# Direction attention: the second scores' banks handed over in pairs of heads, odd jobs between the pairs

## The chip, the cores and the metric

The program runs on one core of one Trainium2 chip, and the metric is the device time of one execution in microseconds. The core has a matrix engine (TensorE, PE in the profile), whose weight loads are a row of their own (PEld), a vector engine (VectorE, DVE), an activation engine (ScalarE, ACT), GpSimd (POOL), and a queue for transfers (SyncE, SP). TensorE writes to PSUM only, here eight banks of 512 fp32 columns on 128 partitions.

## The reference, cut to what matters

The model is four layers, each an attention block and a feed-forward block, each with a residual and a layer norm behind it. Only the attention of layer 1 is touched ("direction attention", `_L1_attn_ref`): 4 batches of 512 tokens, 8 heads, a causal softmax.

```
q3 = (x @ Wq.T).reshape(Bb, Tt, H, 3).transpose(0, 2, 1, 3)
k3 = (x @ Wk.T).reshape(Bb, Tt, H, 3).transpose(0, 2, 1, 3)
v = (x @ Wv.T).reshape(Bb, Tt, H, HD).transpose(0, 2, 1, 3)
scores = einsum('bhtd,bhsd->bhts', q3, k3) * scale + q_on_dir[..., :, None] * k_on_dir[..., None, :]
attn = softmax(where(causal, scores, -inf), axis=-1)
out = einsum('bhts,bhsd->bhtd', attn, v) ... @ Wo.T
```

The head's width for scores is 3, with a fourth product along a fixed direction; for values it is 16.

## The kernel before, in words

Each block is written with one instruction stream per engine, in an order written out by hand; engines wait for each other on semaphores, and each engine runs its stream strictly in the order of the text. Nothing is scheduled by a planner.

The stage is `direction_attention` (line 1749). Its inputs are `q_parts` and `k_parts`: bf16 parts of queries and keys, 32 rows per head, so that four heads fill 128 partitions. The work goes by 8 **units** U (4 batches by 2 groups of 4 heads), each of 4 **steps** k, one for each block of 128 keys; in all 32 steps s. There are two passes over the scores:

- **The first pass** finds the row maxima. It goes head by head (32 heads f, one per step, 7 heads ahead: in step s it is head s + 7). `first_mask` (line 1809) writes the causal mask into bank 0, 512 columns; `first_products` (line 1818) adds four diagonal products, then two long products into bank 1, then two "edge" products into bank 7. VectorE reduces the three in turn (`maxima`, lines 1962, 1964, 1966: "diagonal", "long", "edge"). After every fourth head it splits the maxima into bf16 parts (lines 1970 to 1974).
- **The second pass** makes the probabilities. `second(s)` writes the transposed scores less the maxima of four heads into banks 2 to 5: four products of 32 rows and (4 - k) x 128 columns (line 1851), one per head, then four products of 128 rows and 128 columns that add the mask (line 1854). ScalarE takes them in two exponentials of two banks each (`probabilities(s, 0)` and `(s, 1)`, line 1922), then `values(s)` (line 1865) multiplies by the values, four fp32 products into bank 6.

Three **odd jobs** share bank 7 with the edge products, so each waits until VectorE has reduced the edge of the head before: `spread_sums` (line 1872) in step k = 1, `max_rows` (line 1837) in step k = 2, `out` (line 1878) in step k = 0 of units 3, 5 and 7. `m_read` holds what bank 7 waits for. At the end of a unit ScalarE copies bank 6 out (`copy_y`, line 1928), and the next unit's first values wait for that copy. `less_maxima` (line 1979) makes the next unit's query operand from what `max_rows` wrote.

In step s TensorE runs: `second(s+1)`, `first_mask`, an odd job if there is one, `values(s)`, `first_products`. In the last 7 steps there is no first pass left.

The functions that the change touches, with the line numbers of the profile:

Of the kernel before, what the change touches and what calls it, by code (L numbers as in the profile page):

```python
# [1748 lines left out]
def direction_attention(core, q_parts, k_parts, v_aug, w_out, sum_spread, out_loaded):  # L1749
# [3 lines left out]
    H = 4  # L1753
    n_units = 2 * B
    n_steps = n_units * QT
    n_heads = n_units * H
    LEAD = 7
    with Stage(core, "a1") as st:
# [20 lines left out]
        def diagonal_done(f):  # L1779
            return 3 * f + 1  # L1780

        def long_done(f):
            return 3 * f + 2

        def edge_done(f):
            return 3 * f + 3

        def out_of(s):

            U, k = s // QT, s % QT  # L1790
            return (U - 3) // 2 if k == 0 and U >= 3 and U % 2 == 1 else None

        with nc.Block() as block:
            @block.gpsimd
            def _(pool):
                nc.gpsimd.memset(nparts[:], 0.0).then_inc(zeroed, 1)
                for U in range(n_units):
                    b, g = U // 2, U % 2
                    pool.wait_ge(inv_ready, U + 1)
                    if b > 0:  # L1800
                        pool.wait_ge(out_done, b)
                    nc.gpsimd.tensor_tensor(yn[:, g, :], y[:, g, :], inv_sum[:], ALU.mult).then_inc(yn_ready, 1)

            @block.tensor
            def _(pe):
                def first_mask(f):
                    if f >= 1:
                        pe.wait_ge(top_ready, diagonal_done(f - 1))
                    nc.tensor.matmul(ps_d, core.identb[:], mask_wide[:].rearrange("p q n -> p (q n)"), start=True, stop=False, skip_group_check=True)

                def first_products(f, m_read):

                    U, h = f // H, f % H
                    col, g = (U // 2) * T, U % 2
                    rows = slice(32 * h, 32 * h + 32)

                    def product(to, q, k, n):
                        return nc.tensor.matmul(to, q_parts[rows, g, col + q * P:col + (q + 1) * P], k_parts[rows, g, col + k * P:col + (k + n) * P],
                                                start=k != q, stop=True, skip_group_check=True)

                    for q in range(QT):
                        last = product(ps_d[:, q * P:(q + 1) * P], q, q, 1)
                    last.then_inc(first_ready, 1)
                    if f >= 1:
                        pe.wait_ge(top_ready, long_done(f - 1))
                    product(ps_f[:, 0:2 * P], 2, 0, 2)
                    product(ps_f[:, 2 * P:4 * P], 3, 1, 2).then_inc(first_ready, 1)
                    if m_read is not None:
                        pe.wait_ge(*m_read)
                    product(ps_m[:, 0:P], 1, 0, 1)  # L1830
                    product(ps_m[:, P:2 * P], 3, 0, 1).then_inc(first_ready, 1)

                def max_rows(U, m_read):
                    pe.wait_ge(nparts_ready, U + 1)
                    pe.wait_ge(*m_read)
                    for t in range(QT):
                        last = nc.tensor.matmul(ps_m[:, t * P:(t + 1) * P], nparts[:, t, :, :].rearrange("p h r -> p (h r)"), core.identb[:],
                                                start=True, stop=True)
                    last.then_inc(rows_ready, 1)

                def second(s):
                    U, k = s // QT, s % QT
                    col, g = (U // 2) * T, U % 2
                    size = (QT - k) * P
                    if k == 0:
                        pe.wait_ge(q_ready, U + 1)
                    if s > 0:
                        pe.wait_ge(probs_ready, 2 * (s - 1) + 2)
                    for h in range(H):
                        rows = slice(32 * h, 32 * h + 32)  # L1850
                        nc.tensor.matmul(ps_s[:, h, 0:size], k_parts[rows, g, col + k * P:col + (k + 1) * P], q_less[rows, g, k * P:T],
                                         start=True, stop=False, skip_group_check=True)
                    for h in range(H):
                        last = nc.tensor.matmul(ps_s[:, h, 0:P], core.maskb[:], core.identb[:], start=False, stop=True, skip_group_check=True)
                        if h % 2 == 1:
                            last.then_inc(s_ready, 1)

                def values(s):
                    U, k = s // QT, s % QT
                    b, g = U // 2, U % 2  # L1860
                    pe.wait_ge(probs_ready, 2 * s + 2)
                    if k == 0 and U > 0:
                        pe.wait_ge(y_ready, U)
                    for h in range(H):
                        last = nc.tensor.matmul(ps_y[32 * h:32 * h + 32, k * P:T], v_aug[:, b * QT + k, H * g + h, :], probs_t[:, s % 2, h, 0:(QT - k) * P],
                                                start=k == 0, stop=k == QT - 1, skip_group_check=True)
                    last.then_inc(values_done, 1)

                def spread_sums(U, m_read):
                    pe.wait_ge(y_ready, U + 1)  # L1870
                    pe.wait_ge(*m_read)
                    nc.tensor.matmul(ps_m, sum_spread[:], y[:, U % 2, :], start=True, stop=True).then_inc(sums_ready, 1)

                def out(b, m_read):
                    pe.wait_ge(yn_ready, 2 * b + 2)
                    pe.wait_ge(*m_read)
                    for g in range(2):
                        last = nc.tensor.matmul(ps_m, w_out[:, g, :], yn[:, g, :], start=g == 0, stop=g == 1)
                    last.then_inc(out_done, 1)

                pe.wait_ge(mask_ready, 1)
                pe.wait_ge(out_loaded, 2 * 16)
                m_read = None
                for f in range(LEAD):
                    first_mask(f)
                    first_products(f, m_read)
                    m_read = top_ready, edge_done(f)
                max_rows(0, m_read)
                m_read = q_ready, 1
                second(0)  # L1890
                for s in range(n_steps):
                    U, k, f = s // QT, s % QT, s + LEAD
                    if s + 1 < n_steps:
                        second(s + 1)
                    if f < n_heads:
                        first_mask(f)
                    if out_of(s) is not None:
                        out(out_of(s), m_read)
                        m_read = sum_done, out_of(s) + 1
                    if k == 1 and U >= 1:  # L1900
                        spread_sums(U - 1, m_read)
                        m_read = ln_ready, U
                    if k == 2 and U + 1 < n_units:
                        max_rows(U + 1, m_read)
                        m_read = q_ready, U + 2
                    values(s)
                    if f < n_heads:
                        first_products(f, m_read)
                        m_read = top_ready, edge_done(f)
                spread_sums(n_units - 1, m_read)  # L1910
                out(B - 1, (ln_ready, n_units))
# [642 lines left out]
```

## Time and profile before

| | us |
|---|---|
| median of 3 runs | 1914.7 |
| lowest and highest of them | 1914.29 and 1924.76 |
| the profiled execution, its own time | 1913.05 |
| its span, first to last instruction | 1910.9 |
| mean granted TensorE clock over the span | 0.931 |
| PE busy, share of the span | 87% |
| ACT, DVE, POOL busy | 59%, 58%, 38% |

The span runs from the first to the last instruction of the profiled execution, 2.15 us less than its own time. The shares of busy time are averages over all blocks of the model. The steps of the stage that is changed, from the first to the last of its matmuls in line 1851 and what follows them, lie between 286.6 and about 391 us of the span. A matmul of fp32 operands shows as two records.

### The profile page before, as it was taken

The page shows a single profiled execution, that of the slowest core. Times are in us where ns is not written, and L with a number is a line of the kernel's source. Part 1 is how long each engine was busy: PE and PEld are TensorE (multiplying, and loading weights), DVE is VectorE, ACT ScalarE, POOL GpSimd, SP SyncE. Part 2 cuts the span into 40 slices and gives each one's busy share as a digit, 9 for nine tenths or more (in the row PEclk, how much of TensorE's full clock was granted, in tenths as well). Part 3 has the DMA queues.
Part 4 walks back from the last instruction along what each step waited for, and adds up shares of the span by engine and source line. Part 5 has one row for each costly group of instructions (what it writes and reads, how often), then busy time and mean ns, then how long its engine had stood idle before and what let it go on. Part 6 is the DMA issues. An engine that isn't in the chain of part 4 may idle for free. (4 is left out here: it accounts for less than half of the span.)

```text
span 1910.9 us, 27976 instructions
## 1 busy us (share of the span) xinstructions
PE 1657.7 (87%) x8908; PEld 1061.3 (56%) x8908; DVE 1107.7 (58%) x2224; ACT 1125.7 (59%) x2356; POOL 735.3 (38%) x665
## 2 busy tenths in 40 slices
PE   5558978859999699999869999999989998858898
PEld 3337733328886466666435555555547886323685
DVE  5955675545655455555345555555548886652475
ACT  4324555537777355555456566556538887753687
POOL 1224420122332466666245545555424442001463
PEclk8868979969999899999979999999989999878899
DMA  1007200002121222222211111111117652000321
GB/s 40 1 14 171 65 1 1 1 27 92 73 82 60 54 59 61 56 60 62 67 41 38 45 44 37 43 45 40 29 35 279 221 213 81 1 0 20 111 105 45
DMA packets 54507, 120.43 MB, mean 63 GB/s; under 512 B 12788, under 2 KB 23900, under 8 KB 47196
## 3 DMA queue, kind: packets, MB, share of 16 engines
q1 hardware_dynamic: 54364, 118.68, 20.9%
q8 instruction: 70, 1.15, 0.2%
q14 instruction: 73, 0.60, 0.1%
HBM read 82.99 MB, written 2.10 MB: 45 GB/s over the span
## 5 line engine op out<-in xcount | busy, mean ns | idle before, releaser
L847 DVE TENSOR_TENSOR e_lo<-psum,e_hi 128x512 fp32r<-128x512 f32 x296 | 203.0, 686 | 90.8 <-ACT psum L812 90.7
L1459 ACT ACTIVATE h_probs<-psum,h_nmax 128x512 f32<-128x512 f32 (+3 forms) x256 | 132.6, 523 | 132.7 <-DVE h_nmax L1537 78.1
L1537 DVE TENSOR_REDUCE h_nmax<-psum 128x1 f32<-128x512 f32 (+3 forms) x256 | 113.9, 486 | 118.7 <-PE psum L1348 118.4
L770 PE MATMUL psum<-f_x_hi,f_w_hi 128*128 128x512 f32 x400 | 160.3, 401 | 6.8 <-DVE e_gated L861 4.0
L772 PE MATMUL psum<-f_x_lo,f_w_hi 128*128 128x512 f32 x400 | 158.9, 397 | 0.0
L771 PE MATMUL psum<-f_x_hi,f_w_lo 128*128 128x512 f32 x400 | 158.5, 396 | 0.0
L1274 POOL TENSOR_TENSOR h_swapped<-h_swapped,rope_tables 128x512 f32<-128x512 f32 x64 | 81.7, 1276 | 185.2 <-DMA h_swapped<-h_raw 185.2
L812 ACT ACTIVATE psum<-psum,f_b 128x512 f32<-128x512 f32 x200 | 132.4, 662 | 25.5 <-PE psum L772 25.5
L789 PE MATMUL psum<-e_lo,f_w_hi 128*128 128x512 f32 x364 | 143.8, 395 | 2.2 <-DVE e_lo L847 1.2
L786 PE MATMUL psum<-e_hi,f_w_hi 128*128 128x512 f32 x364 | 143.4, 394 | 0.0
L787 PE MATMUL psum<-e_hi,f_w_lo 128*128 128x512 f32 x364 | 143.1, 393 | 0.0
L1459 ACT ACTIVATE a_probs<-psum,a_nmax 128x512 f32<-128x512 f32 (+3 forms) x128 | 67.4, 527 | 118.1 <-DVE a_nmax L1537 69.5
L738 POOL TENSOR_TENSOR e_lo<-e_gated,e_hi 128x512 fp32r<-128x512 f32 x59 | 76.1, 1289 | 140.0 <-ACT e_hi L824 140.0
L732 POOL TENSOR_TENSOR sum_fm<-e_part,sum_fm 128x512 f32<-128x512 f32 x60 | 77.3, 1288 | 132.2 <-DVE e_part L873 97.3
L1274 POOL TENSOR_TENSOR a_swapped<-a_swapped,a2f_a_tables 128x512 f32<-128x512 f32 x64 | 83.0, 1296 | 109.4 <-DMA a_swapped<-a_raw 109.3
L1345 PE MATMUL psum<-h_k,h_q 64*128 64x384 f32 (+3 forms) x512 | 104.9, 485 | 22.0 <-DVE h_p_t L1546 16.8
L1355 PE MATMUL psum<-ident,h_probs 128*128 128x128 f32 x640 | 109.2, 279 | 0.4 <-ACT h_probs L1459 0.4
L1537 DVE TENSOR_REDUCE a_nmax<-psum 128x1 f32<-128x512 f32 (+3 forms) x128 | 62.6, 489 | 67.6 <-PE psum L1348 66.4
L818 ACT ACTIVATE e_hi<-psum 128x512 fp32r<-128x512 f32 x128 | 76.7, 599 | 39.1 <-PE psum L772 39.1
L1345 PE MATMUL psum<-a_k,a_q 128*128 128x512 f32 (+3 forms) x256 | 91.2, 438 | 6.6 <-DVE a_wvo L1529 6.6
L770 PEld LDWEIGHTS psum<-f_x_hi,f_w_hi 128*128 128x128 f32 x400 | 76.5, 191 | 25.8 <-issue 4.7
L1373 PE MATMUL psum<-h_p_t,h_v 128*64 128x256 f32 (+3 forms) x512 | 89.9, 451 | 0.0
(426 smaller groups left out, 4050.6 us busy)
## 6 DMA issues: line engine op xcount, KB each, us to landing
e_gate<-gates SPq DMA_DIRECT2D x46, 1024.0 KB, 4.7
a_swapped<-a_raw SPq DMA_DIRECT2D x128, 128.0 KB, 2.3
h_swapped<-h_raw SPq DMA_DIRECT2D x256, 64.0 KB, 2.0
e_gate<-gates SPq DMA_DIRECT2D x16, 512.0 KB, 6.7
f_w<-in_l_experts SPq DMA_DIRECT2D x8, 512.0 KB, 5.4
f_w<-in_l_experts SPq DMA_DIRECT2D x32, 128.0 KB, 4.6
e_gate<-gates SPq DMA_DIRECT2D x12, 256.0 KB, 4.2
f_w<-in_l_experts SPq DMA_DIRECT2D x9, 256.0 KB, 4.8
```

What stands on the lines that cost most here:

```text
L770: nc.tensor.matmul(to, w_h, ex.x_hi[:, cols(b)], start=True, stop=False, skip_group_check=True)
L771: nc.tensor.matmul(to, w_l, ex.x_hi[:, cols(b)], start=False, stop=False, skip_group_check=True)
L772: nc.tensor.matmul(to, w_h, ex.x_lo[:, cols(b)], start=False, stop=True, skip_group_check=True).then_inc(hid_ready, 1)
L786: nc.tensor.matmul(to, w_h, hi[:, n % PLACES, :], start=start, stop=False, skip_group_check=True)
L787: nc.tensor.matmul(to, w_l, hi[:, n % PLACES, :], start=False, stop=False, skip_group_check=True)
L789: nc.tensor.matmul(to, w_h, lo[:, n % PLACES, :], start=False, stop=True, skip_group_check=True).then_inc(out_done, 1)
L812: nc.scalar.activation(to, hidden_bank(n), ex.act_func, **bias(n)).then_inc(act_ready, 1)
L847: nc.vector.tensor_tensor(lo[:, n % PLACES, :], whole, hi[:, n % PLACES, :].bitcast(F32), ALU.subtract).then_inc(lo_dve, 1)
L1274: nc.gpsimd.tensor_tensor(swapped[:, j, :], swapped[:, j, :], tables[:, 2 * j + 1, :], ALU.mult).then_inc(sin_ready, 1)
L1345: nc.tensor.matmul(ring[j % RING][:, 0:(q + 1) * P], qs[rows, U % 3, q * P:(q + 1) * P], ks[rows, U % 3, 0:(q + 1) * P], start=True, stop= ...
L1459: nc.scalar.activation(probs[:, j % 4, 0:(q + 1) * P], ring[j % RING][:, 0:(q + 1) * P], ACT.Exp, bias=nmax[:, j % 8:j % 8 + 1], accum_out ...
L1537: nc.vector.tensor_reduce(nmax[:, j % 8:j % 8 + 1], ring[j % RING][:, 0:(q + 1) * P], AX.X, ALU.max, negate=True).then_inc(max_ready, 1)
```

## The change

`second` now takes a pair number p as well: it makes the products and masks of heads 2p and 2p + 1 only, and waits only for the one exponential that read these two banks in the step before. The main loop issues pair 0 at the start of the step, then the odd job, then pair 1, then the values; `first_mask` moves from ahead of the odd job to behind the values, straight ahead of `first_products`. ScalarE's, VectorE's and GpSimd's instructions and waits are unchanged.

```diff
-                def second(s):
+                def second(s, p):
...
-                    if k == 0:
+                    if k == 0 and p == 0:
                         pe.wait_ge(q_ready, U + 1)
                     if s > 0:
-                        pe.wait_ge(probs_ready, 2 * (s - 1) + 2)
-                    for h in range(H):
+                        pe.wait_ge(probs_ready, 2 * (s - 1) + p + 1)
+                    for h in range(2 * p, 2 * p + 2):
                         rows = slice(32 * h, 32 * h + 32)
...
-                    for h in range(H):
+                    for h in range(2 * p, 2 * p + 2):
                         last = nc.tensor.matmul(ps_s[:, h, 0:P], core.maskb[:], core.identb[:], start=False, stop=True, skip_group_check=True)
-                        if h % 2 == 1:
-                            last.then_inc(s_ready, 1)
+                    last.then_inc(s_ready, 1)
...
-                second(0)
+                second(0, 0)
+                second(0, 1)
                 for s in range(n_steps):
                     U, k, f = s // QT, s % QT, s + LEAD
                     if s + 1 < n_steps:
-                        second(s + 1)
-                    if f < n_heads:
-                        first_mask(f)
+                        second(s + 1, 0)
...
+                    if s + 1 < n_steps:
+                        second(s + 1, 1)
                     values(s)
                     if f < n_heads:
+                        first_mask(f)
                         first_products(f, m_read)
                         m_read = top_ready, edge_done(f)
```

TensorE, step k = 1 of a unit, with the odd job `spread_sums`, before (line 1851 with 256 columns is the second pass, 1854 its masks, 1809 the first pass's mask, 1865 the values, 1818 the first pass's products):

```order
L1851 MATMUL psum<-a_q_less,a1w_k_parts 128x256 x4
L1854 MATMUL psum<-identb,maskb 128x128 x4
L1809 MATMUL psum<-a_mask_wide,identb 128x512
L1872 MATMUL psum<-a_y,a1w_sum_spread 128x512
L1865 MATMUL psum<-a_probs_t,a1w_v_aug 32x384 x4
```

The same step now, where the spread of the sums is line 1871 and the values line 1864:

```order
L1851 MATMUL psum<-a_q_less,a1w_k_parts 128x256 x2
L1854 MATMUL psum<-identb,maskb 128x128 x2
L1871 MATMUL psum<-a_y,a1w_sum_spread 128x512
L1851 MATMUL psum<-a_q_less,a1w_k_parts 128x256 x2
L1854 MATMUL psum<-identb,maskb 128x128 x2
L1864 MATMUL psum<-a_probs_t,a1w_v_aug 32x384 x4
L1809 MATMUL psum<-a_mask_wide,identb 128x512
```

Half of the second scores and the 512-column mask stood ahead of the odd job and stand behind it now. Step k = 2 is the same with `max_rows` (line 1837) in the place of the spread.

TensorE, step k = 0 of units 3 and 5, with the output projection `out` as the odd job, as it is now:

```order
L1851 MATMUL psum<-a_q_less,a1w_k_parts 128x384 x2
L1854 MATMUL psum<-identb,maskb 128x128 x2
L1877 MATMUL psum<-a_yn,a1w_w_out 128x512 x2
L1851 MATMUL psum<-a_q_less,a1w_k_parts 128x384 x2
L1854 MATMUL psum<-identb,maskb 128x128 x2
L1864 MATMUL psum<-a_probs_t,a1w_v_aug 32x512 x4
L1809 MATMUL psum<-a_mask_wide,identb 128x512
```

Before, all four products and masks of 384 and 128 columns and the 512-column mask came first, then `out` (line 1878) and the values.

## Rows read from the trace of the kernel before

**Rows 1.** Windows: stretch, us, busy per engine PE, PEld, DVE, ACT, POOL (instructions), granted clock.

```profile
286.60:385.00 98.40, 81.46 (x793) 36.47 (x793) 54.62 (x120) 53.92 (x86) 8.87 (x7) 0.96 0.00 1
...
311.00:323.00 12.00, 10.04 (x107) 4.71 (x106) 8.13 (x19) 6.91 (x11) 1.26 (x1) 1.00 0.01 1
...
385.00:395.00 10.00, 6.26 (x10) 2.15 (x9) 0.69 (x1) 3.11 (x4) 1.26 (x1) 0.71 0.13 31
...
286.60:292.90 6.30, 4.47 (x26) 1.26 (x27) 0.00 (x0) 3.45 (x4) 0.00 (x0) 0.50 0.00 0
```

**Rows 2.** Waits inside the stage, 286.6 to 385: us in total, times, longest.

```profile
ACT a_probs_t L1922 <- PE psum L1854: 52.3, 30, 17.2
...
PEld psum L1851 <- ACT a_probs_t L1922: 9.2, 9, 2.1
...
PE psum L1872 <- DVE a_tops L1966: 4.2, 6, 1.0
...
PE psum L1837 <- DVE a_tops L1966: 3.8, 6, 0.6
```

**Rows 3.** Timeline of one unit: start us, us, engine line op, idle before.

```profile
310.94 0.61 PE L1818 MATMUL psum<-a1w_k_parts,a1w_q_parts 32*128 32x128 bf16 x6
...
311.81 0.40 PE L1854 MATMUL psum<-identb,maskb 128*128 128x128 bf16 x4
...
312.13 1.94 ACT L1922 ACTIVATE a_probs_t<-psum 128x1024 f32<-128x1024 f32 x2 [2.58 <-PE psum L1854]
...
312.80 0.72 PE L1818 MATMUL psum<-a1w_k_parts,a1w_q_parts 32*128 32x128 bf16 x8
...
313.95 0.60 ACT L1928 ACTIVATE a_y<-psum 128x512 f32<-128x512 f32 x1
...
314.12 0.34 PE L1851 MATMUL psum<-a_q_less,a1w_k_parts 32*128 32x384 bf16 x4 [0.61 <-ACT a_probs_t L1922]
...
314.40 0.40 PE L1854 MATMUL psum<-identb,maskb 128*128 128x128 bf16 x4
...
314.63 0.38 PE L1809 MATMUL psum<-a_mask_wide,identb 128*128 128x512 bf16 x1
...
314.94 1.07 PE L1865 MATMUL psum<-a_probs_t,a1w_v_aug 128*32 128x512 f32 x8
...
315.94 0.61 PE L1818 MATMUL psum<-a1w_k_parts,a1w_q_parts 32*128 32x128 bf16 x6
...
317.57 0.42 DVE L1966 TENSOR_REDUCE a_tops<-psum 128x2 f32<-128x256 f32 x1
...
318.14 1.10 PE L1872 MATMUL psum<-a_y,a1w_sum_spread 128*128 128x512 f32 x2 [0.63 <-DVE a_tops L1966]
...
319.16 0.85 PE L1865 MATMUL psum<-a_probs_t,a1w_v_aug 128*32 128x384 f32 x8
...
319.95 0.61 PE L1818 MATMUL psum<-a1w_k_parts,a1w_q_parts 32*128 32x128 bf16 x6
...
322.15 0.38 PE L1837 MATMUL psum<-identb,a_nparts 128*128 128x128 bf16 x4 [0.63 <-DVE a_tops L1966]
...
322.46 0.64 PE L1865 MATMUL psum<-a_probs_t,a1w_v_aug 128*32 128x256 f32 x8
...
323.03 0.61 PE L1818 MATMUL psum<-a1w_k_parts,a1w_q_parts 32*128 32x128 bf16 x6
```

**Rows 4.** Timeline of the last unit: masks, values, output projection.

```profile
374.11 0.40 PE L1854 MATMUL psum<-identb,maskb 128*128 128x128 bf16 x4
...
374.43 0.43 PE L1865 MATMUL psum<-a_probs_t,a1w_v_aug 128*32 128x128 f32 x8
...
376.93 1.94 PE L1878 MATMUL psum<-a_yn,a1w_w_out 128*128 128x512 f32 x4
...
378.80 1.07 PE L1865 MATMUL psum<-a_probs_t,a1w_v_aug 128*32 128x512 f32 x8
```

**Rows 5.** Timeline of the first step, TensorE.

```profile
290.99 1.94 PE L1865 MATMUL psum<-a_probs_t,a1w_v_aug 128*32 128x512 f32 x8
```

## The prediction

> **What bounds the kernel now.** I first read the windows, to see how much time is at stake. The stage takes 98.4 us from its first second-pass product to 385 us [rows 1], 5% of the span; a whole per cent of the kernel (19 us) would be a fifth of it. In a steady 12 us stretch no engine is full: PE is busy 10.0 us, DVE 8.1, ACT 6.9. So order and waits set the pace, not one engine's work.
>
> Then the waits [rows 2]. The largest is ScalarE's, 52.3 us for PE, of which 17.2 lie ahead of its first exponential; it is slack. What matters is where PE stands still. PE waits for exponentials ahead of line 1851 (9.2 us in all), and for DVE's edge reduction ahead of the odd jobs (4.2 and 3.8 us). The change aims at the first kind. The second kind matters more than its size: it tells which loop closes through DVE.
>
> Then the timeline of one unit [rows 3]. Call F0 to F3 the starts of the first products at the end of steps k = 0 to 3. They are at 310.94 (F2), 312.80 (F3), 315.94 (F0), 319.95 (F1), 323.03 (the next F2). So a unit lasts 12.09 us, in pieces of 1.86, 3.14, 4.01 and 3.08 us. Each has a different bound:
> - F2 to F3: PE works through without a wait.
> - F3 to F0: PE waits 0.61 us for both exponentials of 1024, goes on at 314.12 with the second scores, masks, first mask, and starts the values at 314.94. These also need `copy_y`, which ends at 314.55.
> - F0 to F1: the odd job starts at 318.14, 2.20 us after F0, because DVE must finish the edge reduction (317.57 + 0.42). The whole second pass and the first mask lie inside these 2.20 us, under cover of DVE. Then come 1.02 for the spread and 0.79 for the values.
> - F1 to F2: the same 2.20 us, then 0.31 for `max_rows` and 0.57 for the values.
>
> **The cover is what the change gives away.** In the last two pieces everything issued between first products and odd job is free; everything between odd job and next first products adds to the loop DVE edge, odd job, values, first products, DVE. The change moves two things from the free side to the other: pair 1 of the second scores, and the 512-column first mask.
>
> Prices, from rows:
> - Pair of second scores (two products, two masks). The four products of 384 columns start together and their masks follow 0.28 us later (314.12 to 314.40) [rows 3]; the heads run side by side on their own 32 rows, so two products take what four take. With 128 columns fewer at 2.4 GHz, 0.053 us less each time: 0.22 at 256 columns, 0.17 at 128, and 0.33 at 512. Two masks cost one pitch of 0.056 ((0.40 - 0.23) / 3), and from the last mask to the values is 0.15 (374.11 + 3 x 0.056 to 374.43) [rows 4]. So pair 1 costs 0.49 us at 384 columns, 0.43 at 256 and 0.38 at 128.
> - The first mask ahead of the first products: not shown at full clock in this order. From the first mask to the values it is 0.31 (314.63 to 314.94) [rows 3], of which 0.21 is 512 columns at 2.4 GHz. I take 0.31; streaming alone, 0.21, is the lower end.
>
> These gaps hold a switch of the array between 32-row and 128-row work: 384 columns stream in 0.16 us, yet the masks start after 0.28. The Trainium skill (TensorEngine Tiling (Array Packing), Tiling Modes, Key Properties) says that changing the tiling mode drains the TensorEngine. It gives no price. With no drain, pair 1 would cost about 0.21 at 256 columns instead of 0.43, and the sum below would be some 3 us smaller; the gap of 0.12 in the row speaks for the drain.
>
> **The sum, step by step:**
> - F0 to F1: 2.20 + 1.02 + 0.43 + 0.79 + 0.31 = 4.75 for 4.01, +0.74. This holds in units 1 to 5 (unit 0 has no spread; unit 6 no first pass left): 5 x 0.74 = 3.7.
> - F1 to F2: 2.20 + 0.31 + 0.38 + 0.57 + 0.31 = 3.77 for 3.08, +0.69, in units 0 to 5: 4.1.
> - F2 to F3, no odd job: pair 0's masks start where all masks did, at F2 + 0.87, and its exponential at F2 + 1.19. Pair 1 then costs a switch from masks to products (0.11, as 314.94 less 314.63 less 0.21), 0.33, less the two masks that go, and the first mask no longer stands ahead of the values but behind. F3 comes at F2 + 2.2, +0.35.
> - F3 to F0: pair 0 need only wait for the first exponential. But pair 1 and the values still need the second, which ends at F2 + 3.13, where it ended before (ScalarE is not faster), and the values need `copy_y`, which ends at F2 + 3.62. Values at F2 + 3.67 instead of 4.00, then 1.00, then 0.31 for the mask: F0 at F2 + 5.0, as now. So the handover by pairs wins 0.3 to 0.35 us, and the moved mask and the split spend just that: 0 over the two pieces.
> - With `out` as odd job (units 3 and 5) F0 is bound by DVE too: F3 late by 0.35, pair 1 0.49, mask 0.31: +1.15 each, 2.3. `out` itself (1.87, 376.93 to 378.80) [rows 4] does not change.
> - Unit 0, step 1: no odd job; DVE's wait goes and the split comes, 0.
> - The last 7 steps have no first mask to pay. Pair 1 behind the spread costs 0.43, the next unit's operand comes 0.35 later, `out` of unit 7 starts earlier by about 0.45 since it no longer stands behind the exponential of pair 1, and pair 1 behind it costs 0.49; behind the last spread 0.43, and the last exponentials stand behind the logarithm and inverse. Followed through, the last copy comes 0.8 later than with F0 of unit 6 kept fixed.
>
> Together 3.7 + 4.1 + 2.3 + 0.8 = **10.9 us slower**. The profiled execution's own time is 1913.05, which gives 1924.0; it lies 1.65 us below the median of the runs, 1914.7, which would give 1925.6. I say **1925**.
>
> Bounds of the unknown prices: with streaming time alone for pair 1 and mask (0.2 and 0.21), the 13 places with an odd job lose about 0.4 instead of 0.7, in all +6; with 0.2 more for each added switch, two per place, +16. That is 1919 to 1930 around the own time.
>
> **Rivals.**
> - *Nothing changes on balance (1910 to 1917; chance 0.15).* If PE's sequence had more slack than the rows of one unit show, or the second scores' products of the next pair overlap with the odd job, the moved pieces could be hidden. For it: F3 to F0 comes out even. Against it: 0.63 us idle ahead of each odd job in [rows 3], with DVE's edge named, and 8.0 us of such idle time in total [rows 2]; a loop whose wait stands ahead of the odd job can hide nothing behind it.
> - *The exponentials' handover pays (1904 to 1910; 0.08).* ScalarE starts pair 0 of the next step while PE still works for the rest. All 9.2 us of PE's waits for exponentials [rows 2] gone and the split free gives 1913.05 - 9.2 = 1903.8. Against it: four of these microseconds lie in F3 to F0, where the second exponential and `copy_y` still gate the values, and the rest in the first and last steps, gated likewise. Even in full it is half a per cent.
> - *TensorE's clock falls inside the stage (1933 to 1945; 0.08).* This ends beyond a per cent slower. The granted clock was 1.00 in the steady stretch, with PE busy 10.0 of 12 us, and 0.71 just behind the stage, with PE busy 6.3 of 10 [rows 1]. After the change a unit is 13.5 us with nearly the same work, and more of it is small pairs. In a stretch at 0.50 [rows 1] the values of 512 took 1.94 us [rows 5] for 1.07 [rows 3]. PE's own work on the loops of a unit (spread, values, pair, masks, some 6 us of 13.5) would double: 6 us per unit, so from two low units on the whole is beyond 1933. Against it: PE would stand idle about 2.5 us of 13.5 in a unit, for 1.9 of 12.1 now, in pieces of at most 1.1 us.
> - The change does what it says: the order of TensorE's instructions shows it, and no other engine's order moved.
>
> The forecast (1918 to 1930) has 0.69. I put the range at **1913 to 1933**: it takes in both bounds, half of the neutral rival and the start of the clock's fall, and leaves about 2 in 10 out. A per cent (19 us) is about what a measurement tells from no change here, as a single run of before reached 1924.76. Faster by over 1% has 0.02, since no case gets there by its mechanism; slower by over 1% gets the clock and a little of the dearer switches, 0.10; within 1% 0.88.
>
> **What would show it.** In the changed kernel's timeline the distance from F0 to F1 should be about 4.75 and F1 to F2 3.75, the unit 13.4 to 13.5 instead of 12.09; PE's idle time ahead of the odd jobs should grow to about 1.1 us (the mask, and half of the second scores, no longer fill it), with DVE's edge as releaser; its wait of 0.61 for the exponential ahead of line 1851 in step 0 should shrink. F3 to F0 should be about 2.8. The values should start 0.4 us after pair 1's first product. I am wrong if the odd jobs start less than 2.2 us after the first products, if the first mask runs at the same time as the values before it, or if the unit comes out below 12.5 us. Behind the stage everything should only be shifted.

## The result, and the profile after

The changed kernel takes 1957.51 us (median of 4 runs, 1949.45 to 1968.17) against 1915.49 (4 runs): a ratio of 1.0212, 95% interval 1.015 to 1.0274. So it is slower by 2.1%, 42 us, clear of no change, where 10.9 us and a range up to 1933 were forecast. The order's cost was forecast right; TensorE's clock was not.

The profiled execution of the changed kernel took 1953.39 us, 40.3 more than the one of before. From the stage's first second-pass product (line 1851) to the first matmul of the norm behind it (line 213) it is 286.01 to 430.55, 144.5 us, for 286.62 to 392.05, 105.4 us, before. So 39.1 of the 40.3 us lie in the stage.

Windows of the changed kernel, columns as in [rows 1]: the whole stage, then pieces of it.

```profile
286.00:421.00 135.00, 119.44 (x787) 46.14 (x790) 54.61 (x120) 54.52 (x85) 8.16 (x7) 0.70 0.00 1
...
293.50:306.00 12.50, 10.04 (x104) 4.67 (x104) 8.99 (x20) 6.29 (x10) 0.00 (x0) 1.00 0.01 1
...
306.70:344.00 37.30, 33.69 (x191) 12.81 (x189) 14.20 (x30) 12.80 (x20) 2.53 (x2) 0.55 0.00 1
...
344.00:354.00 10.00, 7.54 (x62) 2.98 (x60) 5.21 (x13) 3.51 (x6) 1.26 (x1) 0.99 0.00 0
...
354.00:366.00 12.00, 11.38 (x73) 4.36 (x71) 5.25 (x10) 4.97 (x7) 0.00 (x0) 0.52 0.01 2
```

The granted clock in the stage is 0.70 for 0.96 before. DVE and ACT do the same work as before (54.6 and 54.5 us busy), spread over 135 us. PE's busy time is 119.4 us for 81.5, with the same instructions: they run at 1.2 GHz for over half of the stage. From 293.5 to 306 the clock was full and PE busy 10.04 of 12.5 us, hardly less than before; then it was 0.55 on average up to 344 (it fell first at 306.7 and was full once more for some 3 us from 310), came back for 10 us at 344 (where PE was busy 7.5 of 10), and fell again.

Where the clock is full, the timeline of the changed kernel answers to [rows 3]. First F2 (298.83) to F0 (303.92):

```profile
298.83 0.50 PE L1818 MATMUL psum<-a1w_k_parts,a1w_q_parts 32*128 32x128 bf16 x5
...
299.70 0.29 PE L1854 MATMUL psum<-identb,maskb 128*128 128x128 bf16 x2
...
299.92 0.39 PE L1851 MATMUL psum<-a_q_less,a1w_k_parts 32*128 32x512 bf16 x2
...
300.24 0.28 PE L1854 MATMUL psum<-identb,maskb 128*128 128x128 bf16 x2
...
300.82 0.39 PE L1809 MATMUL psum<-a_mask_wide,identb 128*128 128x512 bf16 x1
...
301.14 0.50 PE L1818 MATMUL psum<-a1w_k_parts,a1w_q_parts 32*128 32x128 bf16 x5
...
302.02 0.34 PE L1851 MATMUL psum<-a_q_less,a1w_k_parts 32*128 32x384 bf16 x2
...
302.60 1.06 PE L1864 MATMUL psum<-a_probs_t,a1w_v_aug 128*32 128x512 f32 x8
...
303.60 0.39 PE L1809 MATMUL psum<-a_mask_wide,identb 128*128 128x512 bf16 x1
...
303.92 0.50 PE L1818 MATMUL psum<-a1w_k_parts,a1w_q_parts 32*128 32x128 bf16 x5
```

F2 to F3 is 2.31 (forecast 2.2, before 1.86) and F3 to F0 2.78 (forecast 2.8, before 3.14). Pair 1's products (302.02) wait for the second exponential, and the values follow 0.58 us behind them, at 302.60, for 0.82 before (314.12 to 314.94) [rows 3]; the mask at 303.60 takes back what that won. Then F0 (346.38) to F1 (351.15), in the next full stretch:

```profile
346.38 0.50 PE L1818 MATMUL psum<-a1w_k_parts,a1w_q_parts 32*128 32x128 bf16 x5
...
348.02 0.42 DVE L1967 TENSOR_REDUCE a_tops<-psum 128x2 f32<-128x256 f32 x1
...
348.58 1.10 PE L1871 MATMUL psum<-a_y,a1w_sum_spread 128*128 128x512 f32 x2 [1.26 <-DVE a_tops L1967]
...
349.61 0.28 PE L1851 MATMUL psum<-a_q_less,a1w_k_parts 32*128 32x256 bf16 x2
...
349.82 0.28 PE L1854 MATMUL psum<-identb,maskb 128*128 128x128 bf16 x2
...
350.04 0.85 PE L1864 MATMUL psum<-a_probs_t,a1w_v_aug 128*32 128x384 f32 x8
...
350.82 0.39 PE L1809 MATMUL psum<-a_mask_wide,identb 128*128 128x512 bf16 x1
...
351.15 0.61 PE L1818 MATMUL psum<-a1w_k_parts,a1w_q_parts 32*128 32x128 bf16 x6
```

These rows show the cover leaving: PE stands idle 1.26 us ahead of the spread (0.63 before), and behind it come pair 1 (349.61), its masks, the values and the first mask (350.82). The piece takes 4.77 us, where 4.75 was forecast and 4.01 was before. The same piece at the lower clock, F0 at 322.82 to F1 at 329.84:

```profile
322.82 0.82 PE L1818 MATMUL psum<-a1w_k_parts,a1w_q_parts 32*128 32x128 bf16 x5
...
324.67 0.41 DVE L1967 TENSOR_REDUCE a_tops<-psum 128x2 f32<-128x256 f32 x1
...
325.23 2.05 PE L1871 MATMUL psum<-a_y,a1w_sum_spread 128*128 128x512 f32 x2 [0.84 <-DVE a_tops L1967]
...
327.21 0.39 PE L1851 MATMUL psum<-a_q_less,a1w_k_parts 32*128 32x256 bf16 x2
...
327.86 1.51 PE L1864 MATMUL psum<-a_probs_t,a1w_v_aug 128*32 128x384 f32 x8
...
329.30 0.61 PE L1809 MATMUL psum<-a_mask_wide,identb 128*128 128x512 bf16 x1
...
329.84 1.03 PE L1818 MATMUL psum<-a1w_k_parts,a1w_q_parts 32*128 32x128 bf16 x6
```

DVE's edge reduction takes 0.41 as ever, but the spread 2.05 for 1.10, the values 1.51 for 0.85, and the piece 7.02. One whole unit at the lower clock (318.16 to 338.79) lasts 20.6 us. No whole unit of the change ran at full clock; in experiment 5, in the same order, it is 13.6.

### The profile page after: what moved, and what is told of

The parts are those of the page before. It is cut to its first block and busy times, and to the rows that moved or that the text cites. A ratio compares the mean times of both kernels' runs of the same rounds, so it can differ in the third digit from the quotient of the medians.

```text
span 1951.2 us, 27976 instructions
## 1 busy us (share of the span) xinstructions
PE 1697.1 (87%) x8908; PEld 1071.3 (55%) x8908; DVE 1109.7 (57%) x2224; ACT 1127.6 (58%) x2356; POOL 736.1 (38%) x665
## 5 line engine op out<-in xcount | busy, mean ns | idle before, releaser
L818 ACT ACTIVATE e_hi<-psum 128x512 fp32r<-128x512 f32 x128 | 76.9, 601 | 39.1 <-PE psum L772 39.1
L1923 ACT ACTIVATE a_probs_t<-psum 128x1024 f32<-128x1024 f32 (+3 forms) x64 | 43.7, 703 | 96.4 <-PE psum L1854 96.2
```

## The experiments

The rule for the stage's length is the one above: from the first product of line 1851 to the first matmul of the norm behind, in the profiled execution. "Unit" is four consecutive pieces without `out`, at full clock; where no whole unit ran so (the change and experiment 6) it is taken from experiments 5 and 9. Ratios are against runs of before on the same chip; the experiments ran on three chips, on which before had medians of 1913.7 to 1916.2.

| kernel | ratio (95%) | stage us | unit | clock in the stage |
|---|---|---|---|---|
| before | | 105.4 | 12.09 | full from 293 on |
| the change | 1.0212 (1.015 to 1.0274) | 144.5 | 13.6 | low most of the time |
| 1 split only | 1.0049 (1.0022 to 1.0076) | 106.6 | 11.98 | full |
| 2 mask only | 1.0021 (0.9993 to 1.0049) | 110.9 | 12.84 | full |
| 3 pair 1 behind only | 1.0146 (1.0094 to 1.0198) | 133.1 | 13.27 | low up to 335, twice later |
| 4 mask also ahead | 1.0153 (1.0105 to 1.0201) | 132.5 | 14.56 | falls for shorter stretches |
| 5 two masks ahead, odd steps | 1.0110 (1.0062 to 1.0159) | 123.6 | 13.62 | low up to 312, then full |
| 6 before, long reduction twice | 1.0177 (1.0121 to 1.0233) | 137.7 | about 13.3 | low and full by turns |
| 7 values ahead of odd jobs | 0.9969 (0.9943 to 0.9996) | 105.0 | 11.27 | full but for one short stretch |
| 8 values ahead, pairs in step 0 | 1.0009 (0.9982 to 1.0035) | 109.5 | 11.26 | low up to 315, then full |
| 9 as 6, two masks ahead | 1.0079 (1.005 to 1.0108) | 117.3 | 13.29 | full |
| 10 as 8, three masks at the start | 0.9967 (0.9933 to 1.0) | 103.6 | 11.26 | full from 293 on |

**1. Only the split.** Pairs 0 and 1 and the first mask all ahead of the odd job.

```diff
                         second(s + 1, 0)
+                        second(s + 1, 1)
+                    if f < n_heads:
+                        first_mask(f)
...
-                    if s + 1 < n_steps:
-                        second(s + 1, 1)
                     values(s)
                     if f < n_heads:
-                        first_mask(f)
```

> Only the handover by pairs: pair 0, pair 1, first mask, then the odd job, values, first products. Everything split stands under cover of VectorE's reductions. Clock theory (the clock fell because moved work left TensorE idle ahead of the odd jobs): idle there about 0.4 us, a unit 12.0 us, the clock in the stage as before, 1912 to 1916. Rival A (two products at a time in place of four are the thinner work that lets the clock fall): 1940 or more with granted clock near 0.5 in the stage. Rival B (the handover itself wins): 1908 to 1912.

The stage is 1.1 us longer, the clock full. Rival A falls: two heads at a time do not bring the clock down by themselves. F2 to F3 is 2.20 for 1.86 and F3 to F0 2.69 for 3.14: the handover by pairs wins 0.11 us per unit, 1% of it, and F0 to F1 and F1 to F2 stay at 4.01 and 3.08, since everything split there is under cover. The runs are 0.5% slower all the same, though not by the stage: of the 10.3 us by which the profiled span is longer, 10.0 lie in the unchanged blocks between 613 and 949 us (335.9 us, for 325.9 before), nearly all at the start of the next attention. Windows of that start, first before, then this kernel:

```profile
650.00:690.00 40.00, 35.04 (x168) 22.64 (x167) 24.64 (x52) 22.33 (x61) 24.46 (x21) 1.00 0.29 65
```

```profile
650.00:690.00 40.00, 31.41 (x126) 19.79 (x125) 23.61 (x38) 17.41 (x48) 19.31 (x15) 0.85 0.21 48
```

The program is the same there; the clock was 1.00 in the one and 0.85 in the other. A difference of 2 to 12 us in this stretch stood in every one of these kernels but the last, so below only the stage's own length is read for small effects.

**2. Only the first mask moved**, from ahead of the odd job to behind the values.

> Only the first mask moved behind the values; four heads at once as before, all ahead of the odd job. At full clock the 13 places with an odd job lose 0.31 us each and the step without one nothing or 0.3: 1918 to 1920. Clock theory: idle ahead of the odd job grows from 0.63 to about 0.95 us; if that alone suffices, the clock falls and the time is 1935 or more. Rival A (thin pairs): no fall, 1918 to 1920.

F0 to F1 is 4.33 and F1 to F2 3.40: +0.32 each, the price taken (0.31). The stage is 5.5 us longer. The clock holds. PE stands idle 1.04 us ahead of the spread and 1.09 ahead of `max_rows`, for 1.26 and 0.63 in experiment 3: more in sum, so the sum of the idle time ahead of the odd jobs does not bring it down, and my expectation of 0.95 us as perhaps enough fails. Nor does PE's busy share. The unit from 304.36 on is busy less than the change was ahead of its first fall (10.04 of 12.5 us), and the clock stays full:

```profile
304.36:317.20 12.84, 9.62 (x105) 4.81 (x107) 8.21 (x18) 6.91 (x12) 1.26 (x1) 1.00 0.01 1
```

**3. Only pair 1 behind the odd job**; the first mask stays ahead.

> Pair 1 behind the odd job, the first mask kept ahead of it. At full clock 0.40 us for each of 13 places, less 0.3 us gained in each step 0: 1917 to 1920. Clock theory: idle ahead of the odd job about 0.85 us; the clock may or may not fall. Rival A: it falls as in the change, 1940 or more.

At full clock F0 to F1 is 4.44 and F1 to F2 3.46, +0.43 and +0.38, as priced. But the clock stays low from the stage's start to 335 us and falls again later; 0.75 over the stage. With 2 this would still fit "the halves, once an odd job stands between them, do it". Experiments 5 and 6 decide that.

**4. The first mask also ahead of the odd job**, in every step; the real one follows and overwrites it.

> The change, with the first mask issued once more ahead of the odd job (it is overwritten by the real one): 25 more matmuls of 512 columns in time in which TensorE stood idle. Clock theory: the clock holds, a unit 13.4 us as worked out for full clock, 1923 to 1927. Rival A and any theory by which the loss is in the order itself: no better than the change, 1950 to 1968.

Neither came out clean. The clock in the stage is 0.86 instead of 0.70, but in the steps without an odd job the added mask stands on PE's own path (F2 to F3 2.72, F3 to F0 3.30), so a unit at full clock is 14.56 us. It points to too little work per time as the cause and does not show it.

**5. Two masks ahead, only in the steps with an odd job**, where PE is idle.

```diff
                         second(s + 1, 0)
+                    if f < n_heads and (out_of(s) is not None or (k == 1 and U >= 1) or k == 2):
+                        first_mask(f)
+                        first_mask(f)
```

> The change, with the first mask issued two more times ahead of the odd job, only in the steps that have one, where TensorE stands idle 1.1 us (both are overwritten by the real one). Clock theory (the stage's work per time is too thin once a unit lasts over 13 us): the clock holds, F0 to F1 4.8 and F1 to F2 3.8 us in every unit, the stage 11 us longer than before, 1924 to 1928. Order theory (the order or the halves of the second scores bring the clock down whatever stands between them): as the change, 1950 or more.

Windows of this kernel, then one piece of its timeline:

```profile
287.60:312.00 24.40, 24.06 (x139) 8.58 (x140) 8.22 (x18) 9.53 (x13) 0.00 (x0) 0.51 0.00 1
...
312.00:400.60 88.60, 79.40 (x664) 32.43 (x660) 46.51 (x102) 43.37 (x69) 7.58 (x6) 1.00 0.00 1
```

```profile
341.94 0.50 PE L1818 MATMUL psum<-a1w_k_parts,a1w_q_parts 32*128 32x128 bf16 x5
...
343.12 0.60 PE L1809 MATMUL psum<-a_mask_wide,identb 128*128 128x512 bf16 x2 [0.24 <-DVE a_tops L1966]
...
344.13 1.10 PE L1871 MATMUL psum<-a_y,a1w_sum_spread 128*128 128x512 f32 x2 [0.41 <-DVE a_tops L1970]
...
346.38 0.39 PE L1809 MATMUL psum<-a_mask_wide,identb 128*128 128x512 bf16 x1
...
346.70 0.61 PE L1818 MATMUL psum<-a1w_k_parts,a1w_q_parts 32*128 32x128 bf16 x6
```

From 312 us on the clock is full to the end of the stage, in the change's own order. F0 to F1 is 4.76 with the two added masks (343.12) in the idle time and at no cost, F1 to F2 3.78, F3 to F0 with `out` 5.89 (5.87 by the prediction's terms). So the order alone does not bring the clock down. By the medians it is 19 us faster than the change with more work in it. Half of my expectation fails: up to 312 us the clock was low, and the stage is 18.2 us longer than before, not 11.

**6. The kernel before, VectorE's long reduction twice**, into a spare tile; TensorE's stream is untouched.

```diff
-                    nc.vector.tensor_reduce(flat[:, bass.ds(9, 4, 2)], ps_f.rearrange("p (n k) -> p n k", k=P), AX.X, ALU.max).then_inc(top_ready, 1)
+                    last = nc.vector.tensor_reduce(flat[:, bass.ds(9, 4, 2)], ps_f.rearrange("p (n k) -> p n k", k=P), AX.X, ALU.max)
+                    if f >= LEAD:
+                        last = nc.vector.tensor_reduce(spare[:], ps_f.rearrange("p (n k) -> p n k", k=P), AX.X, ALU.max)
+                    last.then_inc(top_ready, 1)
```

> The kernel before, TensorE's order and work untouched; VectorE makes the long reduction of each head of the main loop a second time into a spare tile, so every odd job starts 0.6 us later and a unit lasts 13.3 us. Clock theory: the clock falls as in the change, though nothing of the change is in it, 1935 or more. Order theory: the clock holds and the 13 places cost 0.6 us each, 1922 to 1925.

The clock falls, to 0.70 on average over the stage behind its start:

```profile
298.00:411.00 113.00, 97.22 (x685) 40.85 (x682) 63.46 (x131) 47.02 (x74) 7.58 (x6) 0.70 0.00 1
```

Nothing of the change is in this kernel; only the odd jobs start 0.6 us later. The order theory falls. What it shares with the change is a longer unit for the same TensorE work, and with it a longer idle piece ahead of the odd jobs (1.23 us at full clock, for 1.26 in the change). The profiled execution, 1937.54, is the shortest of four (up to 1955.98), so a typical one loses more than these rows show.

**9. The same with two masks ahead of the odd jobs**, as in 5.

> The kernel before with VectorE's long reduction twice, as one experiment earlier, and the first mask issued two more times ahead of each odd job, so in the idle time that the later reduction makes (both are overwritten or rewritten by the same values). Clock theory: the clock holds from the first units on, a unit 13.3 us, the stage 8 us longer than before, 1922 to 1926, so the added matmuls make the kernel faster than without them. Rival (VectorE's double reading of the bank slows the stage by itself): the stage stays as long as without the added matmuls, about 190 us.

```profile
300.00:392.00 92.00, 77.41 (x701) 32.76 (x700) 62.54 (x131) 46.82 (x74) 7.59 (x6) 0.98 0.00 1
```

The clock is 0.98 and the stage 117.3 us instead of 137.7; the median is 1931.03 for 1950.08, 15 and 36 us over the medians of before on their own chips (2 and 1). Matmuls whose result is overwritten make the kernel 19 us faster, and the expectation's rival, that VectorE's second reading of the bank keeps the stage as long, falls. The stage is 11.9 us longer than before, where 8 was expected.

**7. The opposite of the change**: values ahead of the odd job, under cover.

```diff
                         first_mask(f)
+                    values(s)
                     if out_of(s) is not None:
...
-                    values(s)
```

> The kernel before, with the values ahead of the odd job, so under cover of VectorE's reductions, the opposite of the change. If the loop edge reduction, odd job, values, first products is what bounds steps 1 and 2: F0 to F1 3.35 for 4.01, F1 to F2 2.55 for 3.08, given back in part by VectorE's later query operand (F2 to F3 2.2 for 1.86), stage 6 us shorter, 1906 to 1910. If the loop is not the bound: no change of the stage.

```profile
303.89 0.61 PE L1818 MATMUL psum<-a1w_k_parts,a1w_q_parts 32*128 32x128 bf16 x6
...
305.07 0.39 PE L1809 MATMUL psum<-a_mask_wide,identb 128*128 128x512 bf16 x1
...
305.39 0.85 PE L1865 MATMUL psum<-a_probs_t,a1w_v_aug 128*32 128x384 f32 x8
...
306.18 1.12 PE L1872 MATMUL psum<-a_y,a1w_sum_spread 128*128 128x512 f32 x2
...
307.23 0.50 PE L1818 MATMUL psum<-a1w_k_parts,a1w_q_parts 32*128 32x128 bf16 x5
```

F0 (303.89) to F1 (307.23) is 3.34, and F1 to F2 2.52, F2 to F3 2.19, as expected: the loop through VectorE did bound these pieces. But the profiled stage is only 0.4 us shorter, not 6: behind `out` F0 to F1 is 3.61, F3 to F0 with `out` took 6.61 once (5.14 the other time), at a low clock from about 324.7, and from F0 of unit 6 to the norm it is 1.9 us longer. That fall came in the densest order yet, behind a wait of 0.69 us:

```profile
324.62 0.51 PE L1851 MATMUL psum<-a_q_less,a1w_k_parts 32*128 32x384 bf16 x4 [0.69 <-ACT a_probs_t L1922]
```

The kernel is faster by 0.3%, just clear of no change.

**8. Values ahead of spread and output, pairs in step 0 only.**

> Pairs only in step 0, with the first mask between them, and the values ahead of the spread and the output projection but behind max_rows. Loop theory: F0 to F1 3.35 for 4.01, F2 to F0 4.7 for 5.0, F1 to F2 as before, unit 11.1 for 12.09, stage 7 us shorter, 1905 to 1909. If the handover by pairs is worth nothing: F2 to F0 stays 5.0 and the stage is 5 us shorter.

```profile
293.50:315.00 21.50, 21.41 (x136) 9.03 (x134) 10.88 (x26) 7.31 (x12) 0.00 (x0) 0.50 0.00 1
...
315.00:385.00 70.00, 63.14 (x607) 27.59 (x606) 43.65 (x94) 40.16 (x66) 7.60 (x6) 1.00 0.01 1
```

F0 to F1 is 3.34 and F2 to F0 4.84 (1.86 and 2.98; expected 4.7, before 5.00), so pairs with the mask between them are worth 0.16 us per unit. The unit is 11.26 us, but the clock rose only at 315 us, with PE busy 21.4 of 21.5 us, and the kernel wins nothing.

**10. The same with three more first masks** behind the first second scores. The 1.8 us that the expectation names are PE's wait in the kernel before (289.58); in experiment 8, the one to compare with, the handover by pairs had left 0.25 us of it:

```profile
289.42 0.50 PE L1851 MATMUL psum<-a_q_less,a1w_k_parts 32*128 32x384 bf16 x2 [0.25 <-ACT a_probs_t L1928]
```

> Pairs in step 0 only and values ahead of two odd jobs, as one experiment earlier, with three more first masks behind the first second scores, where TensorE waits 1.8 us for the first exponentials. If the longer stretch at 1.2 GHz in the first three units came from thin work at the stage's start: the clock rises by 295 us, the stage is 152 to 154 us long, 1906 to 1910. If it was only where the stage's start fell: no difference to the version without them, 1911 to 1920.

```profile
286.00:293.50 7.50, 7.50 (x40) 2.25 (x40) 0.18 (x1) 3.56 (x4) 0.00 (x0) 0.53 0.00 0
...
293.50:378.00 84.50, 76.17 (x733) 33.24 (x730) 54.27 (x120) 47.30 (x77) 7.58 (x6) 1.00 0.00 1
```

The clock is up from 293.5 on and the median 1907.37 for 1916.20; nine of ten runs lie between 1904.6 and 1910.3 (the tenth is 1926.49), those of 8, on another chip, between 1911.5 and 1927.9. The stage is 103.6 us, 6.0 less than in 8 (of 15.2 us between the two profiled executions) but not the 152 to 154 I had written, which counted the stage from the norm ahead (157.9 by that count; 159.7 before). It is the best of these kernels beside 7, and its interval touches 1.0. What made the clock rise earlier is not shown. The stage's first product came at 285.96 here and at 287.37 in 8, so the expectation's other reading, that it is only where the stage's start falls, still stands.

## Why the prediction was wrong

- **What bounds the stage**: right. Experiment 7 shortens the pieces with an odd job by 0.67 and 0.57 us by taking the values out of the loop, and experiments 2 and 3 lengthen them by what they put in.
- **F0 to F1, F1 to F2**: forecast +0.74 and +0.69; at full clock +0.75 and +0.70 (experiment 5). Split up, the mask cost 0.32 (priced 0.31) and pair 1 0.43 and 0.38 (priced so).
- **F2 to F0**: forecast even, measured 5.09 for 5.00.
- **`out`**: F3 to F0 5.89, forecast 5.87.
- **The last steps**: forecast +0.8, measured +0.9. From F0 of unit 6 to the last spread it is 17.08 us in experiment 5 (385.93 to 403.01) and 16.18 before (368.20 to 384.38).
- **The sum**: with these sizes, 5 x 0.75 + 6 x 0.70 + 4 x 0.09 + 2 x 1.25 + 0.9 = 11.7 us of the 39.1. The other 27.4 us are nearly all the clock: the change's pieces from F0 of unit 1 (303.92) to F0 of unit 6 (404.81), set against the same pieces at full clock in experiment 5, are 26.6 us longer.
- **The step that failed** is the rival "TensorE's clock falls inside the stage", to which the prediction gave 0.08, and with it the assumption under the sum that every duration is one at 2.4 GHz. Its price was right in kind (+6 us per low unit forecast; 20.6 less 13.6, 7.0 measured) and it was given 1933 to 1945; 27.4 us are about four units at 7.0 each, and the profiled execution came to 1953, the median to 1957.5. The argument against it, that PE would stand idle 2.5 us of 13.5 for 1.9 of 12.1, compared two busy shares and took a small difference for a safe one; the idle pieces of at most 1.1 us in it came to 1.26. Nothing in the trace of before says how near the clock was to falling. A rival whose condition can't be read from a trace should have had more than 0.08.
- The neutral rival and the one by which the handover pays are out: experiment 1, the handover with everything under cover, wins 0.11 us per unit. The 9.2 us that this rival set out from are the wait of PE's weight loads; PE's own row for the same exponentials in the same view is 7.0 us.
- Pair 1 at 256 columns came to the 0.43 that had the gap in it, not to the 0.21 of streaming alone (experiment 3, 4.44 for 4.01). The rule of the Trainium skill (TensorEngine Tiling (Array Packing), Tiling Modes) that a change of tiling mode drains the array agrees with that.

What stays open is why the clock held in experiment 2 and not in 3 and 6, whose units are only half a microsecond longer. Experiments 5 and 9 show that matmuls in the idle time keep it up, but they add work and shorten the idle pieces at once, so two readings are left. By one it is the work in a unit's time. By the other it is the length of the single idle piece: ahead of the spread, at full clock, that was 1.26 us in the change, 3 and 4 and 1.23 in 6, where the clock fell, and 0.63 before, 0.82 in 1, 1.04 in 2, 0.80 in 9 and 0.41 in 5, where it held. Neither covers every row: single pieces of 1.47 us (experiment 2, 298.05) and 1.26 us (experiment 5, 388.13) passed without a fall, and experiment 7 has one fall with neither a long unit nor a long piece.

Open too is what sets when the clock rises at the stage's start, 293 us in most kernels, 312 to 335 in experiments 5, 8 and 3. Idle time in the first wait is not it: the kernel before stood idle there for 1.82 us and rose by 293, experiment 8 for 0.25 us and rose at 315.

## What to carry to other kernels

In an engine that runs in order, look what stands between the last instruction that starts another engine and the wait for that engine: it is free, and whatever is moved behind the wait is paid in full, however small the wait looks in the table. And before a stage with small matmuls is made longer with the same TensorE work, reckon with its clock: here 12 us of order brought 27 us of clock with them, and overwritten matmuls in idle time took most of it back.

## What the runs showed that I had not expected

- The clock of TensorE fell in a stage in which PE was busy 10.04 of 12.5 us, and matmuls without a use made a kernel faster: 1931.03 us with them, 1950.08 without (experiments 9 and 6).
- At the low clock PE was nearly always busy (21.4 of 21.5 us in experiment 8) and stayed at 1.2 GHz for over 20 us. So a high busy share in a trace is no sign of a full clock; the granted clock has to be read beside it. The Trainium skill (Trainium Kernel Development and Optimization, Performance Expectations) calls matmul busy time a bad metric for how near a kernel is to its limit, and this row agrees.
- In kernels with identical instructions in a later attention, that stretch took 326 to 338 us. In experiment 1 the 10 us more came with a lower granted clock at its start (0.85 for 1.00 over 40 us).
